# A gated delta-rule scan on one Trainium2 core: the scan's order rewritten, with the attention mask on GpSimd moved ahead of the wait for the solve

## What is computed

```python
normed = (x - mu) * rsqrt(var + LN_EPS) * ln_g + ln_b      # of an already normed x
q, k, v, beta_pre = split(normed @ w_qkvb + b_qkvb, 4)     # 16 heads of 16
beta = sigmoid(beta_pre)
k = k / maximum(norm(k), NORM_EPS)
def step(S, inp):                                          # 512 steps in each of 8 batches
    retrieval = einsum('bhij,bhj->bhi', S, k_t)
    S = S + einsum('bhi,bhj->bhij', beta_t * (v_t - retrieval), k_t)
    return S, einsum('bhij,bhj->bhi', S, q_t)
out = x + scan_out @ w_out + b_out
```

## Time and profile before

| | us |
|---|---|
| median of 3 runs (lowest, highest) | 1049.23 (1046.55, 1050.08) |
| the profiled execution | 1049.88 |
| its span in the trace | 1047.7 |
| prologue, to the first chunk's transposes | 48.7 |
| scan, to the end of the last solve | 638.8 |
| cross-attention, searches and FFN | the rest |

### The profile page before, as it was taken

The page is one execution under the profiler, slowest core; times in us unless marked ns, Lnnn a source line. Parts: engine busy times, 40 slices in busy tenths (PEclk is TensorE's granted clock), DMA queues, the critical chain, the costliest instruction groups (busy, mean ns, idle before and its releaser), DMA issues.

```text
span 1047.7 us, 19435 instructions
## 1 busy us (share of the span) xinstructions
PE 913.1 (87%) x6084; PEld 695.0 (66%) x6091; DVE 885.6 (85%) x2603; ACT 655.9 (63%) x1597; POOL 503.6 (48%) x731
## 2 busy tenths in 40 slices
PE   7899999999999999999999998989999921895066
PEld 7577787778787877877788786766666620442044
DVE  4788899989999999999999998766677787799887
ACT  4576777656667666666666665445677750894085
POOL 5344435533554564455355545245678870970000
PEclk9799999989999999999999999999999975898589
DMA  9800000000000000001200000021420000000012
GB/s 157 141 5 8 6 7 9 9 6 7 8 10 7 6 12 6 7 9 44 92 7 11 7 6 10 20 85 59 162 76 2 1 0 1 1 1 1 1 66 96
DMA packets 28572, 30.49 MB, mean 29 GB/s; under 512 B 5548, under 2 KB 23864, under 8 KB 28472
## 3 DMA queue, kind: packets, MB, share of 16 engines
q1 hardware_dynamic: 28256, 29.12, 11.4%
q10 hardware_dynamic: 216, 0.14, 0.0%
HBM read 20.85 MB, written 4.19 MB: 24 GB/s over the span
## 4 chain that ended last, share of the span: by engine, by line
PE 76%; DVE 17%; issue 4%; ACT 2%; POOL 1%; DVEq 0%; ACTq 0%; POOLq 0%
PE ps L1911 8%; PE ps L1903 7%; PE psG L1865 6%; PE ps L1842 6%; PE psY L1879 5%; PE psX L1879 4%; PE ps L2029 4%; PE psX L1957 4%; PE psY L1957 3%; PE psG L1859 3%; PE psX L2050 2%; PE ps L1971 2%; PE ps L2217 2%; PE psY L2050 2%; PE psG L1860 2%
## 5 line engine op out<-in xcount | busy, mean ns | idle before, releaser
L550 POOL TENSOR_TENSOR arena<-arena 128x256 f32<-128x256 f32 x32 | 23.3, 729 | 304.0 <-DVE arena L1232 304.0
L687 ACT ACTIVATE arena<-ps 128x512 f32<-128x512 f32 x128 | 72.9, 596 | 40.6 <-PE ps L1903 40.3
L1903 PE MATMUL ps<-work 32*128 32x256 f32 x512 | 94.2, 409 | 2.5 <-ACT work L733 1.8
L509 POOL TENSOR_SCALAR_AFFINE_SELECT arena<-arena 128x2048 f32<-128x2048 f32 x32 | 92.1, 2877 | 2.2
L652 ACT ACTIVATE arena<-ps,nparity 32x256 f32<-32x256 f32 x124 | 51.1, 458 | 48.5 <-PE ps L1842 48.1
L1903 PEld LDWEIGHTS ps<-work 32*128 32x128 f32 x512 | 62.7, 188 | 19.8 <-issue 12.0
L1865 PE MATMUL psG<-arena 128*128 128x512 f32 x128 | 75.1, 673 | 0.5 <-DVE arena L1298 0.5
L1243 DVE TENSOR_TENSOR arena<-arena 128x256 f32<-128x256 f32 (+1 forms) x96 | 66.6, 694 | 3.5
L1842 PE MATMUL ps<-work,arena 128*128 128x64 f32 x496 | 62.1, 280 | 7.6 <-DVE work L1258 7.6
L1246 DVE TENSOR_REDUCE arena<-arena 128x64 f32<-128x256 f32 (+1 forms) x96 | 65.9, 687 | 3.3
L1879 PEld LDWEIGHTS psY<-work,arena 128*128 128x128 f32 x512 | 59.8, 195 | 12.0 <-DVE arena L1315 9.9
(11 more groups left out here) (341 smaller groups left out, 2595.9 us busy)
## 6 DMA issues: line engine op xcount, KB each, us to landing
arena<-in_mask_BxSxS_ik SPq DMA_DIRECT2D x8, 1024.0 KB, 6.6
xs<-arena SPq DMA_DIRECT2D x256, 16.0 KB, 1.8
arena<-in_ctx SPq DMA_DIRECT2D x8, 512.0 KB, 4.1
out<-xs SPq DMA_DIRECT2D x32, 128.0 KB, 1.7
arena<-in_x SPq DMA_DIRECT2D x8, 288.0 KB, 19.5
arena<-in_L_ffn_w SPq DMA_DIRECT2D x2, 1024.0 KB, 23.6
arena<-in_x SPq DMA_DIRECT2D x16, 96.0 KB, 7.1
arena<-in_L_attn_w_qkvb SPq DMA_DIRECT2D x2, 512.0 KB, 4.7
```

The source lines that it names most:

```text
L509: G.affine_select(out=pairs, in_=pairs, compare_op=ALU.is_ge, fill=0.0, base=0, pattern=[[0, NH], [-CT, B], [0, CT]], channel_multiplier=1 ...
L687: A.activation(attn[j % 2][:, r * 512:(r + 1) * 512], ps[(2, 0)[r % 2]][:, :], ACT.Copy).then_inc(att_out, 1)
L1903: last = M.matmul(ps[(2, 0)[r % 2]][:, f * 2 * P:(f + 1) * 2 * P], kq[j % 4][rows, f * P:(f + 1) * P], qe[rows, f].rearrange("p e t -> p ( ...
```

## The change

GpSimd: `mask_attention(j)` stands ahead of the wait for `u_done`, so it starts when the fourth part of the attention is copied out. `key_norms` there is a maximum, a power and a copy. The addition of the mixed outputs to x, and the late input statistics, come to GpSimd. VectorE: `scale_far` goes (the far sums are read from PSUM, and beta is multiplied on 128 sums inside the solve), `key_norms` and `x_added` go, `keys_normed` leaves the solve, the transposes are two halves. TensorE: a new order (state, turn, values, key_sums, retrieval, updates_turned, far_gram of the same chunk, attention 0 and 1, outputs(j-1), attention 2 and 3, norms, queries, near_gram of the next chunk, betas and keys, mixed), outputs loops its four column groups innermost, and `kept_busy` issues matmuls without use from chunk 29 on and in the searches and before the FFN's two sets of matmuls. ScalarE: copies for the key sums and the mixed outputs, its early work ahead of the attention copies, two early loads of function tables. The core of the diff:

```diff
-                ss, root, sqr = nrm
-                for n in range(3):
-                    own(G.tensor_tensor(sqr, root, root, ALU.mult))
-                    own(G.tensor_tensor(sqr, sqr, ss, ALU.mult))
-                    own(G.tensor_scalar(sqr, sqr, -0.5, 1.5, ALU.mult, ALU.add))
-                    if n < 2:
-                        own(G.tensor_tensor(root, root, sqr, ALU.mult))
+                ss, root, length = nrm
+                own(G.tensor_scalar(length, ss, NORM_EPS * NORM_EPS, None, ALU.max))
+                own(G.tensor_tensor(root, length, half, ALU.pow))
                 pool.wait_ge(rn_T, m)
-                wide = [t.rearrange("p (h a) -> p h a", a=1).broadcast_to([P, NH, HD]) for t in (sqr, root)]
-                G.tensor_tensor(rn_wide.rearrange("p (h d) -> p h d", d=HD), wide[0], wide[1], ALU.mult).then_inc(rn_ready, 1)
+                G.tensor_copy(rn_wide.rearrange("p (h d) -> p h d", d=HD),
+                              root.rearrange("p (h a) -> p h a", a=1).broadcast_to([P, NH, HD])).then_inc(rn_ready, 1)
+
+            def x_added(j):
+
+                pool.wait_ge(mixed_out, j + 1)
+                pool.wait_ge(xb_ready, j + 1)
+                G.tensor_tensor(xc[:, j, :], xc[:, j, :], mixed_s, ALU.add).then_inc(x_done, 1)
...
             for j in range(NCK):
+                mask_attention(j)
                 pool.wait_ge(u_done, j + 1)
                 pool.wait_ge(xr_ready, j + 1)
                 G.tensor_tensor(xc[:, j, :], xc[:, j, :], bb_s, ALU.add).then_inc(xb_ready, 1)
-                mask_attention(j)
+                if j >= 1:
+                    x_added(j - 1)
                 if j + 3 < NCK:
                     key_norms(j + 3)
+                if j in FACTORS_AT:
+                    late_inputs(FACTORS_AT[j])
                 if j in ROW_NORMS_AT:
                     row_norms(ROW_NORMS_AT[j])
                 if 12 <= j < 16:
                     for p in range(2 * (j - 12), 2 * (j - 12) + 2):
                         bounded_weights(p)
...
+                    if t == 8:
+                        v.wait_ge(g1_mm, 2 * (j + 1))
...
                         n, a = (8, 0) if t == 8 else (4, t // 8)
-                        src = g1 if n == 8 else g2h[:, :, a].rearrange("p h (t s) -> p h t s", s=4)
+                        src = far if n == 8 else g2h[:, :, a].rearrange("p h (t s) -> p h t s", s=4)
                         part = prod[:, 0:NH * n * n].rearrange("p (h t s) -> p h t s", t=n, s=n)
                         sums = red[:, 0:NH * n].rearrange("p (h t) -> p h t", t=n)
-                        own(V.tensor_tensor(part, src,
-                                            C16[:, :, t - n:t].rearrange("p h (a s) -> p h a s", a=1).broadcast_to([P, NH, n, n]),
-                                            ALU.mult))
+                        mult = V.tensor_tensor(part, src,
+                                               C16[:, :, t - n:t].rearrange("p h (a s) -> p h a s", a=1).broadcast_to([P, NH, n, n]),
+                                               ALU.mult)
+                        if n == 8:
+                            mult.then_inc(far_used, 1)
+                            v.wait_ge(far_used, j + 1)
+                        else:
+                            own(mult)
                         own(V.tensor_reduce(sums, part, AX.X, ALU.add))
+                        if n == 8:
+                            own(V.tensor_tensor(sums, sums, beta[j % 4].rearrange("p (h t) -> p h t", t=CT)[:, :, 8:16], ALU.mult))
                         own(V.tensor_tensor(C16[:, :, t:t + n], C16[:, :, t:t + n], sums, ALU.add))
...
             def updates_turned(j):
                 v.wait_ge(s_mm, j)
-                V.transpose(utm, cbuf.rearrange("p (b s) -> p b s", s=96)[:, :, 0:64]).then_inc(ut_ready, 1)
+                for half in range(2):
+                    V.transpose(utm[:, half * CW:(half + 1) * CW],
+                                cbuf.rearrange("p (b s) -> p b s", s=96)[:, 4 * half:4 * half + 4, 0:64]).then_inc(ut_ready, 1)
...
                     updates_turned(j)
-                if exists(j + 1):
-                    scale_far(j + 1)
                 if j == NCK:
                     masked(0)
                     masked(1)
                     least(0)
                     masked(2)
                     least(1)
-                if exists(j - 1):
-                    x_added(j - 1)
                 if exists(j + 1) and j + 1 < NCK - 1:
                     keys_turned(j + 1)
                 if exists(j + 1):
+                    scale_near(j + 1)
                     state(j + 1)
-                if exists(j + 3):
-                    key_norms(j + 3)
+                    fold_near(j + 1)
+                    far_products(j + 1)
                 if j == 11:
                     ternary_factors()
-                if exists(j + 1):
-                    scale_near(j + 1)
                 if exists(j + 2):
-                    far_products(j + 2)
-                if exists(j + 2):
+                    keys_normed(j + 2)
                     near_products(j + 2)
                 if exists(j + 1):
-                    if j in FACTORS_AT:
-                        late_inputs(*FACTORS_AT[j])
                     start_chunk(j + 1)
...
                 for b in range(NH // 2):
+                    if b % 4 == 0:
+                        pe.wait_ge(ut_ready, 2 * j + 1 + b // 4)
...
-                for r in range(4):
-                    for f in range(DC):
-                        for e in range(2):
+                for f in range(DC):
+                    for e in range(2):
+                        for r in range(4):
...
+            def kept_busy(into, n):
+
+                for _ in range(n):
+                    M.matmul(into[:, 0:P], ones[:, :], ones[:, :], start=True, stop=True)
...
                         state(j - 1)
+                if j >= 1 and exists(j + 3):
+                    turn(j + 3)
+                if j >= 2 and exists(j):
+                    pe.wait_ge(oT_ready, j - 1)
+                    pe.wait_ge(c_ready, j - 1)
+                    values(j)
+                if j >= 1 and exists(j + 2):
+                    key_sums(j + 2)
                 if j >= 1 and exists(j):
-                    near_gram(j)
                     retrieval(j)
                 if exists(j - 1):
                     updates_turned(j - 1)
@@ -2101,41 +2130,41 @@
                     context_whole(1, 0)
                     context_whole(1, 1)
                     pe.wait_ge(ctxT_ready, 4)
-                for f in range(2):
-                    if exists(j):
-                        attention(j, 2 * f)
-                        attention(j, 2 * f + 1)
-                    if exists(j + 1) and j >= 1:
-                        far_gram(j + 1, f)
-                    if f == 0 and exists(j + 2) and j >= 1:
-                        norms_turned(j + 2)
-                if j == 0:
-                    far_gram(1, 0)
-                    far_gram(1, 1)
+                if exists(j):
+                    far_gram(j, 0)
+                    far_gram(j, 1)
+                    attention(j, 0)
+                    attention(j, 1)
                 if exists(j - 1):
                     outputs(j - 1)
+                if exists(j):
+                    attention(j, 2)
+                    attention(j, 3)
+                if exists(j + 2) and j >= 1:
+                    norms_turned(j + 2)
                 if exists(m):
                     pe.wait_ge(att_out, 4 * j + 3)
                     queries(m)
                     if j == 0:
                         norms_turned(2)
                     pe.wait_ge(att_out, 4 * j + 4)
+                elif exists(j + 1):
+                    pe.wait_ge(att_out, 4 * j + 3)
+                    kept_busy(ps[2], 4)
+                if exists(j + 1):
+                    near_gram(j + 1)
+                if j < NCK <= m:
+                    pe.wait_ge(att_out, 4 * j + 4)
+                    kept_busy(ps[0], 7)
+                if exists(m):
                     betas(m)
                     if j == 0:
                         values(1)
                     keys(m)
                 if exists(j - 1):
                     mixed(j - 1, m)
-                if exists(j + 1) and j >= 1:
-                    pe.wait_ge(oT_ready, j)
-                    pe.wait_ge(c_ready, j)
-                    values(j + 1)
                 if j == 11:
                     ternary_sums()
```

More of the change, by code:

```diff
@@ L209, in decoder @@
         third = at[0]
-        G1, G2, G3, G4 = take(1024), take(512), take(512), take(128)
+        G2, G3, G4 = take(512), take(512), take(128)
         prod = take(1024)
+        take(1024)
         red = take(128)
@@ L220, in decoder @@
         nT += [take(D).rearrange("p (c t) -> p c t", c=DC) for _ in range(2)]
+        mixed_s = take(D)
         assert at[0] <= ARENA - NT * D, at[0]
@@ L558, in _ @@
                         bounded_weights(p)
```

(25 more changed lines are left out.)

118 lines of the change are left out of this document (60 added, 58 removed).

## The result

The changed kernel takes 1228.66 us (median; 1218.49 to 1231.34) beside 1048.05 us of the kernel before: 1.170 of it, 95% interval 1.167 to 1.174. The forecast was 1138, in a range of 1010 to 1200. Slower was right, by a good half of the size: 90 us were forecast and 180 came.

The account below looks back on a forecast made before the run. VectorE was taken to set the 20.64 us period; 18.8 + 4.2 + 0.9 = 23.9 us, so 1049.9 + 97.8 + 3 - 12 = 1138.7, given as 1138 us on the median, range 1010 to 1200.

Parts of the forecast that it names:

- The period without the mask, 18.8: Scan chunk: state, its copies, retrieval, start_chunk and solve sum to 18.5 to 18.9 us, taken as 18.8, without the moved mask.
- the quarter, 0.6: TensorE's outputs: by the skill's independent array tiles, its 2.46 us would fall to about a quarter, an estimate of 0.6.
- The lock, 4.2: Second half of the solve: GpSimd's early selects stall VectorE's operations with two SBUF inputs, 4.2 us a chunk, bounds 0 to 5.2.
- The rival that a select doesn't hold a tensor-tensor: Solve: selects don't hold its products, or VectorE keeps them out; period 18.8 to 19.3, 990 us; chance 0.17.
- The clock, 0.9: TensorE idles before each state, so its clock falls in each chunk, costing 0.9 us, range 0 to 3.4.
- Rival (b): Scan: lock, and half clock for most of the chunk; cadence 25.5 to 26.4, 1187 to 1213 us; chance 0.10.
- (a): Scan: lock, but the clock stays full; cadence 23.0, 1112 us; chance 0.16.
- (d): Scan: gain and lock cancel because only one select meets the solve; 18.8 + 1.8, about 1045 us; chance 0.03.
- Elsewhere, -12: Outside the periods: unstretched masked operations, FFN warm-up matmuls and a shorter prologue save 12 us, range 4 to 18.
- 3 less 3.6: Scan's end: the last solve's mask adds 3 us; the masked operations lose their select neighbours, 2.0 + 1.6 us.

Follow-up runs that it names:

- the kernel with the pieces: The changed kernel with each of the two selects, still early, cut by heads into four of 128x512: 1193.00 us, 1.132.
- the old order: The kernel before with one edit, the mask moved ahead of the wait for the solve's end: 1175.62 us, 1.121.
- the kernel with 17 matmuls: The changed kernel with 17 matmuls without use behind mixed in chunks 1 to 28, filling TensorE's wait for the solve: 1128.08 us, 1.076.
- the kernel with the mask late: The changed kernel with the mask alone put back behind the wait for the solve's end, behind x_added: 1048.39 us, 1.000.
- the fills: The changed kernel with the mask put back late and five GpSimd fills of 128x1024 in the mask's early place: 1046.83 us, 0.998.
- the run with powers: The changed kernel with the mask put back late and powers of 128x16 and 128x8 in its early place: 1046.39 us, 0.996.

## Why the prediction was right in direction and wrong in size

**The period without the mask, 18.8: right.** 18.82 where the locks are nearly out of the way, and TensorE's outputs at 1.08 us instead of the 1.2 estimated; the quarter, 0.6, wasn't reached.

**The lock, 4.2: right, its parts less so.** 1.59 + 2.58 = 4.17 in the reading of 1.88 and 2.87 against 0.29, 3.99 with the clock held; period 22.83 for the 23.0 forecast. The selects start 14.4 us behind the solve's end at the full clock, as worked out (14.3 to 15.5). The reckoning had one reduction get through beside each select. None did in the chunk shown: the first select met the last 0.24 us of a reduction, and behind it two operations of 0.29 us each waited one select out. The sum came out as forecast all the same, which is in part luck. Reductions do keep their 0.29 and 0.42 us where they fall beside selects, as in the kernel with the pieces. That the price doesn't depend on the place in the solve doesn't hold in the old order, where a chunk lost 2.7 us. The rival that a select doesn't hold a tensor-tensor is out. One reading of the old trace was too wide: in the earlier trace rows the stretched operation has one SBUF input, so of the two only the earlier trace rows is a case of the rule for two SBUF inputs.

**The clock, 0.9 with a range to 3.4: the step that failed.** It measured 4.4 us in most chunks, and 3.4 on the mean of the 30 periods (26.80 less 23.43 with the 17 matmuls). I took its price from waits of 2.0 to 2.3 us, with 3.41 or 6.83 us at half behind them, and argued that values and turn would hide much of it. Here TensorE waited 3.4 to 4.5 us in every chunk, and the half level lasted 10.24 us, 24 times in the scan. That stretch holds the chain from the first third of the state to most of retrieval: against the kernel with 17 matmuls 1.1 us on the state, 0.8 on turn, values and key_sums, which now end behind the copies and hide nothing, and 2.5 on retrieval. The upper bound was wrong in the same way, as it took the longest stretch seen in the old trace for the longest there is.

The miss is 91 us, and 87 of it lie in the periods, 30 x (26.80 - 23.9). 74 of these are the clock's, 30 x (3.37 - 0.9), and 13 are left with the clock held, as those periods have a mean of 23.43 and not 23.0 (the first is 31.7 us, the last 26.8). Rival (b), with 1187 to 1213, was nearest, though the half level doesn't hold for most of the chunk. (a), at 1112, is the kernel with 17 matmuls, which took 1128. (d) was summed wrongly: 18.8 + 1.8 = 20.6 us gives some 1040 us and not 1045.

Put together from the runs: the new order without the early mask is worth 47 us (1048.05 to 1000.68, with the additions moved as well), the lock costs 127 (1000.68 to 1128.08), the clock 101 (1128.08 to 1228.66).

**Elsewhere, -12: about right by luck, and given back.** The prologue gave 8.2 us where I had 2, and the cross-attention and the FFN together 2.6 where I had 6 for the FFN's warm-up. The first period grew from 23.05 to 29.7 us; with the new order it takes 25.1 to 32.4 in all kernels, so most of that isn't the mask's doing. From the last transposes to the cross-attention it took 5.4 us more, where I had 3 less 3.6: the last chunk has its lock and 13.65 us at half clock.

**What the prediction didn't say** is that the old place has a lock of its own in the new order. It called the early mask useless because nobody waits for it, which holds, but not what the late one would cost: 2.2 us a chunk on fold_near, which is why the experiment that puts it back only equals the kernel before.

What stays open: in 5 of 30 chunks of the changed kernel the half level lasted 3.41 us and the period was 24.0, with the same wait of 4.22 us ahead as in their neighbours. Nor does the length of the wait set the length of the stretch: in the kernel with the pieces waits of 2.1 to 2.8 us were mostly followed by 10.24 or 13.65 us at half, and in the kernel with the mask late most waits of 1.34 us by none, but three by 10.24 or 13.65. No run here tells why.

## What to carry to other kernels

Before an operation is moved to an idle engine or to an idle time, list what the other engine runs beside it: a select or an addition on GpSimd next to VectorE operations with two SBUF inputs cost here up to its own length (4.2 us for two selects of 4.95), next to reductions, transposes or PSUM reads next to nothing (0.07 us for two additions). The cheap places were there, 46 us below the kernel before, and were found by the operands, not by who waits. And a stall of one engine that makes TensorE wait in every chunk is to be priced with the clock that follows, over the whole chain behind it. The stretches that followed single waits in the old trace were no upper bound for it.

## What the runs showed of the hardware

- A select of 128x2048 holds VectorE's 128x128 operations with two SBUF inputs until 0.1 to 0.2 us behind its end; powers of 128x16 (2.9 us) and fills of 128x1024 (0.95 us each) hold nothing. The Trainium skill (SBUF — State Buffer, Who interferes with whom) says that a GpSimd instruction which only writes doesn't contend, and the fills agree with it. By its rule the powers, which read SBUF, would hold the port; the run with powers doesn't agree, and it decides here.
- The lock is symmetric and goes by who starts first: the second select took 3.74 us for 2.88 behind a product of 128x1024, a power 4.01 for 2.93, and a cut select lets about one operation through for each piece.
- Four column groups in the innermost loop bring 32 matmuls of 128x128 by 32 columns from 2.46 to 1.08 us.
- In the scans of the kernel before, the changed one and those with the mask moved or cut, half clock lasted 3.41, 6.83, 10.24 or 13.65 us, mostly around a TensorE wait of 1.3 to 5.5 us before the state, and not always longer with a longer wait.
